# Expert outputs added into two sums in DRAM, one for even and one for odd slots, joined by POOL

## What is computed

```python
probs = softmax(h @ gate_w.T)
top_vals, top_idx = top_k(probs, 2); top_vals /= top_vals.sum(-1)
out_e = silu(h @ gate_proj[e].T) * (h @ up_proj[e].T) @ down_proj[e].T     # 8 experts
x = x + gb * (rw[..., e] * out_e).sum(e)                                   # two experts for each token
h = layernorm(x) * (1 + ca) + sa                                           # layer 1 begins
x = x + ga * tuple_mixer(h)
```

## Time and profile before

| | us |
|---|---|
| median of 3 runs | 2075.51 |
| lowest, highest | 2071.73, 2076.31 |
| the profiled execution | 2070.9 |
| its span, first to last instruction | 2069.1 |
| TensorE busy | 1830.8 (88%) |
| DVE busy | 1233.4 (60%) |
| POOL busy | 713.2 (34%) |
| ACT busy | 687.4 (33%) |

### The profile page before, as it was taken

The page is one execution under the profiler, slowest core; times in us unless marked ns, Lnnn a source line. Parts: engine busy times, 40 slices in busy tenths (PEclk is TensorE's granted clock), DMA queues, the critical chain, the costliest instruction groups (busy, mean ns, idle before and its releaser), DMA issues.

```text
span 2069.1 us, 25147 instructions
## 1 busy us (share of the span) xinstructions
PE 1830.8 (88%) x8300; PEld 1429.5 (69%) x8300; DVE 1233.4 (60%) x2171; ACT 687.4 (33%) x1321; POOL 713.2 (34%) x606
## 2 busy tenths in 40 slices
PE   8999999999999999976657687866589999999996
PEld 5557888888888888765546565535478778787784
DVE  4557666666666666777633233369947565657564
ACT  2433545444454544432111121123341222222220
POOL 1435211212121212112333333436744454436342
PEclk9999999999999999997568898988789999999998
DMA  6211454545454535222568777530200101001011
GB/s 229 82 62 58 134 152 132 153 132 153 132 153 132 153 119 147 70 87 61 193 185 281 203 206 192 117 97 26 61 26 6 52 28 47 12 25 51 6 51 41
DMA packets 83647, 219.73 MB, mean 106 GB/s; under 512 B 6396, under 2 KB 30988, under 8 KB 81008
## 3 DMA queue, kind: packets, MB, share of 16 engines
q1 hardware_dynamic: 59616, 166.85, 25.2%
q0 software_dynamic: 11616, 28.98, 6.3%
q10 hardware_dynamic: 12336, 22.89, 3.8%
HBM read 128.11 MB, written 90.59 MB: 106 GB/s over the span
## 4 chain that ended last, share of the span: by engine, by line
PE 62%; DVE 17%; DMA 12%; issue 5%; ACT 2%; POOL 1%; ACTq 0%; POOLq 0%; DVEq 0%; SPq 0%
PE bank L706 19%; PE bank L708 18%; PE bank L707 18%; DMA u_d<-yt,sm 11%; PE bank L772 2%; PE bank L897 2%; DVE hh L1945 2%; PE bank L992 1%; DVE st L1437 1%; DVE rr L1706 1%; PE bank L737 1%; DVE na L1419 1%; DVE na L1418 1%; DVE fl L1923 1%; DVE xw L1492 1%
## 5 line engine op out<-in xcount | busy, mean ns | idle before, releaser
L1706 DVE RECIPROCAL rr<-rr 128x256 f32<-128x256 f32 x128 | 218.7, 1730 | 4.7 <-ACT num L1175 4.7
L706 PE MATMUL bank<-hT,W1b 128*128 128x512 f32 x512 | 209.4, 409 | 10.3 <-DVE hh L1900 10.3
L706 PE MATMUL bank<-W1a,hT 128*128 128x512 f32 x512 | 209.6, 409 | 3.4 <-DVE hT L1620 3.4
L707 PE MATMUL bank<-hT,W1b 128*128 128x512 f32 x512 | 204.1, 399 | 0.0
L708 PE MATMUL bank<-hT,W1b 128*128 128x512 f32 x512 | 203.9, 398 | 0.0
L708 PE MATMUL bank<-W1a,hT 128*128 128x512 f32 x512 | 201.8, 394 | 0.0
L707 PE MATMUL bank<-W1a,hT 128*128 128x512 f32 x512 | 201.0, 393 | 0.0
L2037 POOL TENSOR_TENSOR x<-x,tmp 128x512 f32<-128x512 f32 x64 | 101.3, 1582 | 260.8 <-DVE tmp L1698 260.8
L1900 DVE TENSOR_TENSOR hh<-hh,bank 128x512 f32<-128x512 f32 x64 | 43.2, 686 | 187.5 <-PE bank L708 157.7
L1725 DVE SCALAR_TENSOR_TENSOR kt<-bank,kt 128x256 fp32r<-128x256 f32 x128 | 50.8, 397 | 174.2 <-ACT vt L1191 174.0
L1965 POOL TENSOR_TENSOR W<-stage,W 128x1024 fp32r<-128x1024 f32 x32 | 76.8, 2400 | 189.6 <-ACT W L1083 187.3
(11 more groups left out here) (263 smaller groups left out, 4581.8 us busy)
## 6 DMA issues: line engine op xcount, KB each, us to landing
hs_d<-bor SPq DMA_DIRECT2D x24, 1548.0 KB, 11.6
WB<-ws_d SPq DMA_DIRECT2D x8, 3072.0 KB
ws_d<-W SPq DMA_DIRECT2D x18, 1024.0 KB, 6.4
stage<-wa SPq DMA_DIRECT2D x32, 512.0 KB, 6.4
stage<-wbe SPq DMA_DIRECT2D x24, 512.0 KB, 4.9
stage<-wdn SPq DMA_DIRECT2D x24, 512.0 KB, 3.9
mw<-wmod SPq DMA_DIRECT2D x10, 1024.0 KB, 4.9
hg<-hs_d ACTq DMA_DIRECT2D x39, 258.0 KB
```

The lines of the kernel that those rows point to most:

```text
L706: pe.matmul(o, lhs(HI), rhs(HI), start=start, stop=False, **kw)
L707: pe.matmul(o, lhs(HI), rhs(LO), start=False, stop=False, **kw)
L1706: dve.reciprocal(rr[:, pair, h], rr[:, pair, h]).then_inc(r_rec, 1)
```

## The change

The sum `u_d` becomes a list of two. Slots with even i are added into `u_d[0]`, which begins with x as before, those with odd i into `u_d[1]`, which begins with zeros: `begin_sum` writes them, four times 1 MB and the 128 spare rows. `us_done` becomes two semaphores, so `add_out(i)` waits for add i-2 (for i under 2: for all of both sums to be begun). `tokens(i)` waits for add i-4 and `weighted(i)` for add i-2, of the same parity. POOL issues the gather of slot i+2 ahead of `add_out(i)`. In `back` SyncE reads both sums, the odd one into `odd0` and `odd1`, which lie over `W1a` and `W1b`, after waiting for TensorE's last use of the expert weights; POOL adds them up tile by tile (`joined`, 16 tiles of 128x512), blocks 0 and 1 at once, block b+2 between the low parts and the gated add of block b. DVE's statistics of a block wait for the join of the block; ACT waits for all joins ahead of the first new weights of stage D.

```diff
-    u_d = nc.dram_tensor("u_d", (P + NB * S, H), F32, kind="Internal").ap()
+    u_d = [nc.dram_tensor(f"u{i}_d", (P + NB * S, H), F32, kind="Internal").ap() for i in range(2)]
...
                 if b == 0:
-                    sp.dma_start(u_d[0:P, :], bor[:, :]).then_inc(ud_stored, 16)
+                    for i in range(2):
+                        sp.dma_start(u_d[i][0:P, :], bor[:, :]).then_inc(ud_stored, 16)
+                sp.dma_start(u_d[1][P + b * S:P + (b + 1) * S, :].rearrange("(t p) n -> p t n", p=P),
+                             bor[:, :].unsqueeze(1).to_broadcast([P, NT, H])).then_inc(ud_stored, 16)
...
             def back():
-                sp.wait_ge(us_done, 16 * SLOTS)
+                sp.wait_ge(dn_full, SLOTS)
+                for i in range(2):
+                    sp.wait_ge(us_done[i], 16 * ((SLOTS + 1 - i) // 2))
                 for b in range(NB):
...
+                    sp.dma_start(odd[b], u_d[1][rows, :].rearrange("(t p) n -> p t n", p=P)).then_inc(odd_back[b], 16)
...
                 if b >= 2:
+                    act.wait_ge(x_sum, NB * NT)
                     split_d(0, 2 * b - 4)
...
-                        dve.wait_ge(x_back[b], 16)
+                        dve.wait_ge(x_sum, NT * (b + 1))
...
                     if i >= 4:
-                        dve.wait_ge(us_done, 16 * (i - 3))
+                        dve.wait_ge(us_done[i % 2], 16 * (i // 2 - 1))
...
                     if i >= 2:
-                        dve.wait_ge(us_done, 16 * (i - 1))
+                        dve.wait_ge(us_done[i % 2], 16 * (i // 2))
...
                     pool.wait_ge(y_evac, i + 1)
-                    pool.wait_ge(us_done, 16 * i) if i > 0 else pool.wait_ge(ud_stored, 16 * (NB + 1))
-                    pool.indirect_dma_start(out=u_d[:, :],
+                    if i >= 2:
+                        pool.wait_ge(us_done[i % 2], 16 * (i // 2))
+                    else:
+                        pool.wait_ge(ud_stored, 16 * (2 * NB + 2))
+                    pool.indirect_dma_start(out=u_d[i % 2][:, :],
...
                 for i in range(SLOTS):
-                    add_out(i)
                     if i + 2 < SLOTS:
                         gather_gates(i + 2)
+                    add_out(i)
+
+            def joined(b):
+                pool.wait_ge(x_back[b], 16)
+                pool.wait_ge(odd_back[b], 16)
+                for t in range(NT):
+                    xt = x[:, b * NT + t, :]
+                    pool.tensor_tensor(xt, xt, odd[b][:, t, :], ALU.add).then_inc(x_sum, 1)
 
             def back():
+                joined(0)
+                joined(1)
                 for b in range(2):
                     ln_out((2, b), 0)
                     ln_out((2, b), 1)
+                    joined(b + 2)
                     gated_add(b)
```

More of the change, by code:

```diff
@@ L299, in over_h1, with over_odd @@
             return a("before_h1", [P, 6144]), a("h1", [P, NT, HP])
-        ((W1a, W2, _, W1b), WB, (_, xw), (_, mw, prow), (_, x0), (_, h1)) = shared(
-            [weights, lambda a: a("WB", [P, 2, 2, 3072], F32R), over_w2, over_mods, over_x0, over_h1])
+        def over_odd(a):
+            return a("odd0", [P, 2 * NT, H]), a("between_odd", [P, 4112]), a("odd1", [P, 2 * NT, H])
+        ((W1a, W2, _, W1b), WB, (_, xw), (_, mw, prow), (_, x0), (_, h1), (odd0, _, odd1)) = shared(
+            [weights, lambda a: a("WB", [P, 2, 2, 3072], F32R), over_w2, over_mods, over_x0, over_h1, over_odd])
         hold2 = sb("hold2", [P, 12304])
@@ L342, in build @@
         hb = [xnb[:, :].rearrange("p (t n) -> p t n", t=NT), h1[:, :, :], h2[:, 0, :, :], h2[:, 1, :, :]]
+        odd = [(odd0, odd1)[b // 2][:, (b % 2) * NT:(b % 2 + 1) * NT, :] for b in range(NB)]
         mrow = stage[:, 0, :].rearrange("p (k n) -> p k n", k=2)
@@ L466, in build @@
         gb_full = [sem(f"b_slot_gates_gathered{i}") for i in range(2)]
-        us_done = sem("b_slot_out_added")
+        us_done = [sem(f"b_slot_out_added{i}") for i in range(2)]
+        odd_back = [sem(f"b_odd_sum_loaded{b}") for b in range(NB)]
+        x_sum = sem("b_sums_joined")
         x_back = [sem(f"b_x_loaded{b}") for b in range(NB)]
@@ L555, in begin_sum @@
                 if b == 0:
-                    sp.dma_start(u_d[0:P, :], bor[:, :]).then_inc(ud_stored, 16)
+                    for i in range(2):
+                        sp.dma_start(u_d[i][0:P, :], bor[:, :]).then_inc(ud_stored, 16)
+                sp.dma_start(u_d[1][P + b * S:P + (b + 1) * S, :].rearrange("(t p) n -> p t n", p=P),
+                             bor[:, :].unsqueeze(1).to_broadcast([P, NT, H])).then_inc(ud_stored, 16)
                 sp.wait_ge(ring_done, RING[("tail", "A", GA - 1, b)] + NT)
-                sp.dma_start(u_d[P + b * S:P + (b + 1) * S, :].rearrange("(t p) n -> p t n", p=P),
+                sp.dma_start(u_d[0][P + b * S:P + (b + 1) * S, :].rearrange("(t p) n -> p t n", p=P),
                              x[:, b * NT:(b + 1) * NT, :]).then_inc(ud_stored, 16)
@@ L666, in back @@
             def back():
-                sp.wait_ge(us_done, 16 * SLOTS)
+                sp.wait_ge(dn_full, SLOTS)
+                for i in range(2):
+                    sp.wait_ge(us_done[i], 16 * ((SLOTS + 1 - i) // 2))
                 for b in range(NB):
-                    sp.dma_start(x[:, b * NT:(b + 1) * NT, :],
-                                 u_d[P + b * S:P + (b + 1) * S, :].rearrange("(t p) n -> p t n", p=P)) \
+                    rows = slice(P + b * S, P + (b + 1) * S)
+                    sp.dma_start(x[:, b * NT:(b + 1) * NT, :], u_d[0][rows, :].rearrange("(t p) n -> p t n", p=P)) \
                         .then_inc(x_back[b], 16)
+                    sp.dma_start(odd[b], u_d[1][rows, :].rearrange("(t p) n -> p t n", p=P)).then_inc(odd_back[b], 16)
             def step_c(b):
@@ L2201, in add_out @@
                                             in_=yt[:, i % 2, :], in_offset=None,
-                                            compute_op=ALU.add).then_inc(us_done, 16)
+                                            compute_op=ALU.add).then_inc(us_done[i % 2], 16)
                 for stored in (row_stored[R_GA0], row_stored[R_GB0]):
```

## The result

The changed kernel takes 2052.18 us (median of 4 runs, 2048.77 to 2054.96), the kernel before beside it 2073.62 us: a ratio of 0.9895, 95% interval 0.9874 to 0.9917. That is 21 us off, where the forecast was 44. The profiled span fell from 2069.1 to 2050.9 us, 18.2 us, and this difference can be divided at two marks that both traces show: `weighted` of slot 0 and of slot 38.

The account below looks back on a forecast made before the run. The prediction took the slot loop to be bound by ordered adds into the sum, then by TensorE and DMA work: 48 us off the loop, 4 on behind it, 44 off in all, giving 2031 us, range 2000 to 2056.

Parts of the forecast that it names:

- the forecast's own 2015 to 2045: Whole kernel: the main case, 30 to 60 us off, chance 0.65.
- the second rival: Slot loop: each load stalls slots as long as now, only quiet steps gain; 29 us off, 2046, chance 0.12.
- Quiet stretches return to 4.85 us: Slot loop between weight loads: the wait for adds goes, so steps fall from about 6.15 to TensorE's 4.85 us.
- What is lost a load: Slot loop beside weight loads: the add lands about 13 us after the load's issue, losing 3 to 4 us a load.
- the second count: Slot loop, counted by waits: 184 + 6 x 4 + 6 for the long burst is 214 us, a gain of 52.
- the sum, 48 off 266.4: Slot loop: the gain taken was 48 us, with 30 and 82 as ends.
- The DMA engines' work as the bound: Slot loop: 192 to 201 us of DMA work against TensorE's 184; gain 53 at share 0.95, 40 at 0.88.
- the two counts: Slot loop: the gain by DMA work, 40 to 53 us, and the gain by waits, 52 us.
- The rival with the same stalls beside a load: Slot loop: gather and add share POOL's queue, so load stalls stay; 29 us off, 2046, chance 0.12.
- Beginning the second sum at no cost: Ahead of the slots: loads queued behind the zeros are wanted several us later; counted 0, kept 0 to 4 us.
- Behind the slots: After the last slot: second read-back and POOL's joins add 4 us, between 1 and 12.
- `gated_add`(0) held up by `joined`(2): Behind the slots: 6.2 us more on POOL before `gated_add`(0); 2.7 covered, 3.5 show in DVE's normalisation of b = 1.

Follow-up runs that it names:

- e3: The changed kernel, two sums kept, with add i again waiting for add i-1 and going ahead of the gather: 2087.64 us, ratio 1.0075 to the kernel before.
- e9: The kernel of e5 (more buffers, two sums) with add i waiting for add i-1 again: 2089.71 us, ratio 1.0075 to the kernel before.
- e7: The changed kernel with POOL issuing add_out(i) ahead of the gather of slot i+2, as before the change: 2047.88 us, ratio 0.9874 to the kernel before.
- e5: The changed kernel with 8 sm, 4 yt, 4 gbt and 6 hg buffers, token numbers and gathers three slots ahead: 2015.71 us, ratio 0.9730 to the kernel before.
- e2: The changed kernel with the second sum's zeros written 60 us earlier, at the beginning of attention's last group: 2048.63 us, ratio 0.9879 to the kernel before.
- e8: The changed kernel with blocks 1 to 3 of the odd sum joined by accumulating DMAs, not POOL instructions: 2039.84 us, ratio 0.9837 to the kernel before.
- e6: The changed kernel with POOL's 16 joins cut from 512 to 8 columns, read-backs and waits kept: 2039.98 us, ratio 0.9845 to the kernel before.

## Why the prediction came out as it did

The measured 2052 lies in the range (2000 to 2056), but near its slow end and outside the forecast's own 2015 to 2045; it is in the range only because that was drawn wide enough for the second rival. The direction and the reason for the gain between loads were right, the size was half. By its own steps:

- **Quiet stretches return to 4.85 us: right.** 1186.72 to 1191.57 and most steps outside the loads. e3 and e9 show that this is the order's doing alone.
- **What is lost a load: mis-sized, and it is the largest miss.** The forecast let an add land 13 us behind the load and lost 3 to 4 us a load. It lands 16.0 us behind: 1.0 us because it is issued later, gather first (e7), 1.9 because the transfer takes 13.2 us in place of 11.3. The forecast took the transfer from the earlier trace rows, where one add is in flight at a time; a second one beside it makes it 1.8 us longer (e7 against e3). Two steps around a load lose 9.2, 8.2, 7.2 and 8.1 us in the four later ones. Over all loads with `winout` 48 us are lost (231.9 - 184) where the second count had 30 and the sum, 48 off 266.4, had 34: 14 of the missing 23 us are here.
- **The DMA engines' work as the bound: wrong as the reason.** It gave nearly the same number, so the two counts seemed to confirm each other, but e5 runs the loop in 196.5 us with the same bytes. The work there is 0.90 x 202 = 182 us, where the forecast had 192 and 201; that it sets the pace of a stretch as soon as it exceeds TensorE's time was not borne out (19.00 of 19.00 us busy at a share of 1.02). The rival with the same stalls beside a load was nearest, 2046 (its 30 x 1.15 makes 34.5 and not 33, so rather 2045); its reason, the shared queue, holds only in part (e7), its effect does: two steps around a load take 0.8 us less than before the change, where the forecast had 3 to 4.
- **Beginning the second sum at no cost: probably wrong.** Slot 0 is 5.5 us later in the change's profile and 1.2 to 5.2 in those of the other kernels with its front, for which 0 to 4 had been kept; how much of that is the zeros, e2 leaves open. The step that failed is "wanted several us later": the rows of block 2 were in only 0.5 us before DVE took them, and the time to landing was there to be read.
- **Behind the slots: right in kind, 10 in place of 4,** inside the bounds of 1 to 12. The read-back and the first join came as priced (odd block 8.2 us after the first issue, join 4.93 us for the 6.21 taken), and nearly all of both was covered (e8). The rest was DVE slowed beside POOL, which stood only in the upper end. The step priced in its place, `gated_add`(0) held up by `joined`(2), was covered.

As for the Trainium skill's round-robin rule ("DMA: Bandwidth & Descriptors", section "Queues, rings and completion order"): an add of 256 KB beside a 3 MB load takes much the same time whether it stands behind a gather (13.2 us) or before it (13.4), so the trace agrees that it shares with the load, and does not show that its neighbour in POOL's queue takes its turns. The add did land later than forecast, as the prediction drew from the rule, but not by the order that it named.

A tile of line 1508 takes 2.50 / 4 = 0.63 us beside joins of 8 columns (e6), 1.15 beside `gated_add` (e8) and 1.69 beside a join. The rule of the Trainium skill that DVE instructions with two SBUF inputs contend with a POOL instruction that reads SBUF ("SBUF — State Buffer", section "Who interferes with whom") agrees with these rows.

## What to carry to other kernels

If a chain of transfers is cut in two, ask at once for the next wait on the same transfers, the reuse of buffers, and set it against the slowest landing and not the common one: here two sums won 21 us, and 36 more came from giving four tiles twice the buffers. An engine's idle time is not free if its work slows a neighbour: POOL's joins made the part behind the slots 10 us longer, most of it by slowing DVE, and accumulating DMAs in their place gave that back. Before a transfer is put into a queue for no cost, read how long before its use the one behind it lands.

## What was not expected of the hardware

- Beside POOL's 128x512 additions two DVE instructions on 128x4 values took 1.23 and 1.19 us, 0.17 without: nearly the length of one of POOL's tiles (4.94 / 4 = 1.24 us). Beside `gated_add` in e6 the same two took 0.76 and 1.19.
- Adds through one queue that are in flight together lengthen each other beside a load (by 1.8 us, e7 against e3), but do not exclude each other: those that the changed kernel issued at 1165.70 and 1170.61 took 13.2 and 10.2 us and so landed 1.9 us apart, less than the 4.7 us that the fastest add takes. In e5 they landed in up to 16.0 us beside a load, and TensorE was still busy 95% of the loop.
- A direct DMA that reads 1 MB from DRAM and accumulates into SBUF landed in 13.3 us (median of three, in flight together with the read-backs), and POOL spent no addition on it.
